# A one-core attention and mixture-of-experts kernel: the front reordered, small products grouped, half units and the last tiles in another order

## What is computed

```python
q, k, v = xn @ Wq.T + bq, xn @ Wk.T + bk, xn @ Wv.T + bv
qk = q @ k.T                                    # per batch, 1024 x 1024
theta = 0.5 + 0.2*sigmoid(qk) + 0.15*tanh(qk) + 0.1*relu(qk)
s = (softmax(theta) @ v) @ Wo.T + bo
e = argmax(xn @ Wr + br)                        # one of 8 experts for each row
y = gelu(xn @ W1[e] + b1[e]) @ W2[e] + b2[e]    # 256 -> 1024 -> 256
out = x + s * silu(y)
```

## Time and profile before

| | us |
|---|---|
| median of 3 runs | 537.14 |
| lowest and highest | 536.58, 537.76 |
| the profiled execution's own time | 537.1 |
| its span | 535.4 |
| TensorE busy in the span | 517.5 |
| VectorE, ScalarE, GpSimd busy | 408.2, 335.2, 195.4 |

### The profile page before, as it was taken

The page is one execution under the profiler, slowest core; times in us unless marked ns, Lnnn a source line. Parts: engine busy times, 40 slices in busy tenths (PEclk is TensorE's granted clock), DMA queues, the critical chain, the costliest instruction groups (busy, mean ns, idle before and its releaser), DMA issues.

```text
span 535.4 us, 10760 instructions
## 1 busy us (share of the span) xinstructions
PE 517.5 (97%) x3779; PEld 484.8 (91%) x3779; DVE 408.2 (76%) x810; ACT 335.2 (63%) x611; POOL 195.4 (36%) x230
## 2 busy tenths in 40 slices
PE   7998999999999999999999979999999999999996
PEld 6888899899989999899999969988899988999996
DVE  6897688955758855498555688758999999777896
ACT  3488778535536634266334464678777887877882
POOL 2226337931222212322112222004577685343443
PEclk9999999999999999999999999999999999999999
DMA  8942920027314731145311421005123232211121
GB/s 279 352 160 99 353 81 1 1 51 245 118 60 131 233 111 39 60 131 206 138 39 39 130 72 40 22 21 184 56 97 106 73 118 90 61 48 41 60 61 59
DMA packets 40323, 57.09 MB, mean 107 GB/s; under 512 B 3607, under 2 KB 35358, under 8 KB 39726
## 3 DMA queue, kind: packets, MB, share of 16 engines
q1 hardware_dynamic: 35020, 45.62, 25.5%
q0 software_dynamic: 3488, 9.47, 6.1%
q10 hardware_dynamic: 1762, 1.32, 0.8%
HBM read 40.68 MB, written 17.56 MB: 109 GB/s over the span
## 4 chain that ended last, share of the span: by engine, by line
PE 83%; DVE 8%; ACT 5%; issue 2%; DMA 2%; ACTq 0%; POOL 0%; POOLq 0%; DVEq 0%
PE ps L855 25%; PE ps L857 24%; PE ps L856 24%; PE ps L954 5%; DVE stats L1316 1%; PE ps L1137 1%; PE ps L1021 1%; DMA row<-xn_rows,unit_token 1%; ACT hid L731 1%; PE ps L1011 1%; DVE theta L1374 1%; DVE theta L1370 1%; DMA xn_all<-in_L_attn_x_dram 1%; ACT theta L618 1%; ACT theta L608 1%
## 5 line engine op out<-in xcount | busy, mean ns | idle before, releaser
L855 PE MATMUL ps<-v_hi,pT_hi 128*128 128x258 f32 x256 | 76.4, 298 | 2.2 <-issue 0.8
L856 PE MATMUL ps<-v_lo,pT_hi 128*128 128x258 f32 x256 | 72.4, 283 | 0.0
L717 ACT ACTIVATE hid<-ps,b_now 128x256 f32<-128x256 f32 x128 | 53.6, 471 | 30.0 <-PE ps L857 29.1
L857 PE MATMUL ps<-v_hi,pT_lo 128*128 128x258 f32 x256 | 72.2, 282 | 0.0
L1370 DVE SCALAR_TENSOR_TENSOR theta<-tanh_s,theta 128x512 f32<-128x512 f32 x64 | 48.8, 763 | 20.7 <-ACT tanh_s L609 20.0
L618 ACT ACTIVATE theta<-theta,neg_max 128x512 f32<-128x512 f32 x64 | 42.9, 721 | 29.9 <-DVE neg_max L1374 29.8
L855 PE MATMUL ps<-w_hi_even,hidT_h 128*128 128x256 f32 x200 | 58.1, 290 | 3.2 <-DVE hidT_l L1658 3.2
L739 ACT ACTIVATE g_sb<-y_sb 128x512 f32<-128x512 f32 x20 | 12.6, 632 | 71.7 <-DVE y_sb L1663 71.7
L499 POOL COPY unit_token<-sorted_token 128x2 int32 x19 | 3.7, 195 | 147.1 <-PE ps L1137 147.1
L857 PE MATMUL ps<-w_hi_even,hidT_l 128*128 128x256 f32 x200 | 56.6, 283 | 0.0
L856 PE MATMUL ps<-w_lo_even,hidT_h 128*128 128x256 f32 x200 | 56.6, 283 | 0.0
(11 more groups left out here) (248 smaller groups left out, 1648.6 us busy)
## 6 DMA issues: line engine op xcount, KB each, us to landing
w_raw_odd<-in_L_ffn_W_dram SPq DMA_DIRECT2D x10, 1024.0 KB, 5.7
w_raw_even<-in_L_ffn_W_dram SPq DMA_DIRECT2D x6, 1024.0 KB, 6.5
sorted_g<-g_sb SPq DMA_DIRECT2D x20, 256.0 KB, 2.2
xn_rows<-xn_all SPq DMA_DIRECT2D x4, 1024.0 KB, 6.1
x_tile<-in_L_attn_x_dram SPq DMA_DIRECT2D x32, 128.0 KB, 2.2
out_dram<-g_tile SPq DMA_DIRECT2D x32, 128.0 KB, 1.7
xn_all<-in_L_attn_x_dram SPq DMA_DIRECT2D x3, 1024.0 KB, 12.4
kept_xT<-passing_xT SPq DMA_DIRECT2D x2, 1024.0 KB, 4.1
```

The lines of the kernel that those rows point to most:

```text
L717: last = nc.scalar.activation(hid[:, j % 2, c * UNIT:(c + 1) * UNIT], ps[:, HID_BANK + j, c * UNIT:(c + 1) * UNIT], ACT.Gelu, bias=b1_now[ ...
L855: mm(dst, a_hi, b_hi, start=first, stop=False)
L856: mm(dst, a_hi, b_lo, start=False, stop=False)
L857: return mm(dst, a_lo, b_hi, start=False, stop=last)
```

## The change

**Front.** The three loads of the bias rows go from SyncE's queue to the head of ScalarE's. TensorE transposes the bias rows first and then does the eight identity products. A bias column (bk) is put beside Wk, so that M's product, 257 columns wide, gives the key offsets too (`offset_products` goes). `kappa` is a product and sum on VectorE over two rows that are loaded broadcast (`bq_all`, `bk_all`). `bo` is loaded broadcast, halved on GpSimd and added on VectorE, in place of a product. `first_u` starts u of the first half of batch 0 with the high parts, then the low part of M, then turns tiles 4 to 7, then the low part of xn. ScalarE normalises tiles 4 and 5 and copies woT and bv_wide, all of which VectorE did.

**Groups.** `route` is done for four tiles at once, `turn` two rounds at once, `invert` four tokens' tiles at once. The products themselves are the same.

**Half units.** The kept halves have semaphores of their own (`act_kept`, `dve_kept`). The hidden layer is handed over in four quarters instead of three pieces, and the high parts of the last two quarters are made on ScalarE. In all units, the wait for the next expert's weights (`w1_split`) moves from ahead of the branch into `hidden` and `half_rows`.

**Around tile 8.** Its exponentials move into `tile_8`, ahead of the last unit's gelus, with two table loads, and VectorE takes `thetas(9)` ahead of the last unit's bias.

**The end.** Tiles 30 and 31 join `ROUTING`. VectorE takes both halves of `thetas(31)` ahead of `transposed_parts(30)`, and TensorE puts the transposes of tile 31, in another bank, between the two halves of `values(30)`.

```diff
@@ constants, SyncE, ScalarE
-    ROUTING = (3, 4, 5, TPB)
+    ROUTING = (3, 4, 5, TPB, NT - 2, NT - 1)
-            for first, src in ((BQ, bq), (BK, bk), (BV, bv)):
-                sp.dma_start(bias_rows[first:first + DC, :], src.rearrange("(c p) -> c p", p=P)).then_inc(small_in, 16)
+            for kept, src in ((bq_all, bq), (bk_all, bk)):
+                sp.dma_start(kept[:, :], src.rearrange("(a d) -> a d", a=1).to_broadcast([P, D])).then_inc(pairs_in, 16)
...
+            for first, src in ((BQ, bq), (BK, bk), (BV, bv)):
+                act.dma_start(bias_rows[first:first + DC, :], src.rearrange("(c p) -> c p", p=P)).then_inc(small_in, 16)
             act.dma_start(wq_raw[:, :, :], chunked(Wq)).then_inc(wqk_in, 16)
@@ TensorE: groups
@@ -931,8 +974,9 @@
-                    if routed_batch is not None:
-                        route(routed_batch, 2 * q + i)
+                if routed_batch is not None and q % 2:
+                    for t in range(2 * q - 2, 2 * q + 2):
+                        route(routed_batch, t)
@@ scores
-                        if turned_batch is not None:
-                            turn(turned_batch, 2 * h + k)
+                        if turned_batch is not None and k == 0:
+                            turn(turned_batch, 2 * h)
+                            turn(turned_batch, 2 * h + 1)
@@ values
-                    if routed_batch is not None:
-                        route(routed_batch, i)
+                    if routed_batch is not None and i % 4 == 3:
+                        for t in range(i - 3, i + 1):
+                            route(routed_batch, t)
@@ TensorE: front
-            for ec in range(DC):
-                mm(ps[:, PT_BANK, 0:D], bv_wide[:, ec, :], woT[:, ec, :], start=ec == 0, stop=False)
-            mm(ps[:, PT_BANK, 0:D], ones[0:1, :], bo_row[:, :], start=False, stop=True).then_inc(const_done, 1)
...
+            for ec in range(DC):
+                last = mm(ps[:, PT_BANK, 0:D], bv_wide[:, ec, :], woT[:, ec, :], start=ec == 0, stop=ec == DC - 1)
+            last.then_inc(const_done, 1)
...
                 if n < 3:
-                    pe.wait_ge(turned_kept, 4 * n + 4)
+                    pe.wait_ge(turned_kept, 4 * n + 3)
...
-            values(n - 2, inverted=[[i] for i in range(TPB)], limited="ends")
-            values(n - 1, inverted=[[TPB + 2 * i, TPB + 2 * i + 1] for i in range(TPB)], limited="full")
+            values(n - 2, inverted=[range(i - 3, i + 1) if i % 4 == 3 else () for i in range(TPB)], limited="ends")
+            values(n - 1, inverted=[range(TPB + 2 * i - 2, TPB + 2 * i + 2) if i % 2 else () for i in range(TPB)], limited="full")
@@ ScalarE: half units
-                for s in range(1, 4):
-                    first, stop = HALF_STEPS[s]
-                    act.wait_ge(hid_done, u * 4 + 3 + stop // 8)
-                    for c in range(first, stop):
+                for s in range(4):
+                    act.wait_ge(hid_done, u * 4 + 3 + s // 2)
+                    for c in range(2 * s, 2 * s + 2):
...
+                wait_apart(act, act_kept, u * 2 + 2)
+                for s in range(2, 4):
+                    nc.scalar.activation(hidT_h[:, 2 * s:2 * s + 2, 0:P], half_gelus(s), ACT.Copy).then_inc(gelu_done, 1)
@@ ScalarE: tile 8
                 for h in range(2):
                     acts(TPB, h)
+                nc.scalar.activation(warm[:, 2:3], zeros[:, 0:1], ACT.Exp)
+                exps(TPB)
@@ TensorE: experts, the end
-                    if c == HC // 2:
-                        pe.wait_ge(w1_split, split)
+                    if c % (HC // 2) == 0:
+                        pe.wait_ge(w1_split, split - 1 + c // (HC // 2))
...
-                pe.wait_ge(w1_split, split - 1)
                 with pe.If(u0 < full):
...
-            weighted(NT - 2)
+
+            pe.wait_ge(half_s_ready, NT - 3)
+            values(NT - 2, blocks=range(0, TPB // 2))
+            pe.wait_ge(acts_done, (NT - 1) * 2)
             transposes(NT - 1)
+            values(NT - 2, blocks=range(TPB // 2, TPB))
             weighted(NT - 1)
@@ VectorE
-            biased(last_u, 1)
             thetas(TPB + 1)
+            biased(last_u, 1)
```

270 lines of the change are left out of this document (137 added, 133 removed).

## The result

The changed kernel takes 539.23 us (median of 20 runs, 536.77 to 541.09). The kernel before takes 536.90 us in the same comparison (20 runs, 536.36 to 537.76). The ratio is 1.0038, with a 95% interval from 1.0029 to 1.0047: slower by 2.3 us, where 5.6 us faster was forecast.

A forecast was written before the change was run, and what follows sets the result against it. TensorE was taken as the bound, so gains could come only from its few waits. Terms -2.1 (up to 66 us), -1.9, -0.9 and -0.8 sum to -5.7 us: 537.1 becomes 531.4, taken as 531.5, range 529.3 to 534.3.

The forecast's parts named there:

- The end, -0.8: Tiles 30 and 31: earlier `thetas(31)` brings `values(31)` to 528.1 instead of 528.86, despite a 0.75 us wait; -0.8 us.
- Half units, -1.9: Three uncovered half units: ScalarE's casts save 0.6 us at each of two, the moved wait 0.7 behind the third.
- lets TensorE start 0.7 us sooner: Behind the third half unit: branch done beforehand, first half's low part ready at 320.9, of a 1.08 us wait.
- Front, -0.4: Kernel start: first product at about 4.2 us, M 1.4 us late, yet `u_product(0, 2)` at 16.6 instead of 17.00.
- the front gives back: Rival: later first product keeps TensorE at its lower clock, M ends 11.5, nothing gained to 47 us; 532.8, chance 0.17.
- const -0.6: Constant: the product with `bo` goes, saving 0.62 us on TensorE; GpSimd's halving takes its place.
- tiles 0 to 2 -1.0: Up to 66 us: tile 2's turning at 45.6, gaps at `values(0)` and `values(1)` 0.4 us each, +0.1 at tile 3.
- Groups, 0.0: Small products: entering a group saves what leaving costs, 0.11 us each, so grouping gains nothing; ends +0.7 and -1.0.
- Behind the experts, -0.9: Around tile 8: the wait for `values(8)` goes, the second, ahead of `transposes(10)`, keeps its length but begins sooner; -0.9 us.
- ScalarE is the new bound: Rival, half units and tile 8: casts wait, table loads delay the last unit; -0.6 and 0.0, so 533.6; chance 0.12.

The follow-up runs named there:

- c4: Kernel before with the new end alone (tiles 30 and 31): 538.16 us against 536.94, ratio 1.0027.
- c1: Changed kernel with the whole front of the kernel before, `bo`'s product included: 538.10 us against 536.94 for the kernel before.
- c2: c1 with the last expert's loop on TensorE beginning at slot 128 of a code block instead of 0: 535.25 us against 536.94 before.
- a1: Changed kernel with Wq ahead of the bias rows, router loads on SyncE, broadcasts behind x's first batch: 537.62 us against 537.00 before.
- a2: a1 plus TensorE's old order at the start, and VectorE's bias-row copies behind its first statistics: 537.67 us against 537.00 before.
- a3: Changed kernel with the wait for the next expert's weights back ahead of the branch: 540.85 us against 537.00 before.
- e3: Kernel before with the changed front alone (loads, warm-up, first u products, offsets, constant): 539.15 us against 536.63.
- d1: Kernel before with the small products in groups alone: 535.30 us against 536.78, ratio 0.9969.
- e1: d3 with the last half unit's two casts back on VectorE: 532.82 us against 536.63 for the kernel before.
- c3: Kernel before with the new half units alone, the weights' wait staying ahead of the branch: 541.94 us against 536.94.
- f2: Kernel before with only the three bias-row loads moved to the head of ScalarE's queue: 541.76 us against 537.05.
- d3: c2 with the old end (tiles 30 and 31 as before): 534.01 us against 536.78 for the kernel before.
- e4: Kernel before with new half units, weights' wait inside the loop, last expert's loop at slot 128: 536.56 us against 536.63.
- d4: Kernel before with only the last expert's loop placed at slot 128 instead of 0: 536.68 us against 536.78.

## Why the prediction was wrong

- **The end, -0.8: it cost 1.2.** On TensorE the step was right: two waits became one, of 0.27 us where 0.75 was expected, and the last product gained 1.2 us between `transposes(10)` and the end. What failed is that I counted up to `values(31)` only. I never priced GpSimd, whose last product hangs on the end of `values(30)`: it moved 1.6 us later in c4 and 3.3 in the changed kernel, and with it the close of the program. I had no row for the drain, only the distance between GpSimd's last product and the span's end, 6.4 us, which I did not look at. Behind TensorE's last product the changed kernel loses 2.5 us, twice what it won ahead of it.
- **Half units, -1.9: the first two nearly as said, the third lost.** The second wait of 0.5 us is gone in both, which is worth 0.47 and 0.45 us (0.6 each forecast), and 0.30 us more are won at the first wait of the third. The step that failed is "lets TensorE start 0.7 us sooner". The 1.08 us of issue was put down to the wait for weights and a branch behind it. The limit was the fetch of the loop's block: c1 and c2 show it. The first half's low part was ready at 319.5, sooner than the 320.9 that I counted, and the unit still started at 321.69, as late as before. In place of a gain of 0.7 us came half clock, which cost 2.5 us in this profile. I had no rival for that. The branch is done beforehand, as I said, where no fetch stands in the way: in c2 the unit starts 0.1 us behind the split.
- **Front, -0.4: it was +3.0 at `u_product(0, 2)`.** The bias rows landed at 5.2 us and not at 4.2: the third load was issued by 1.97 us, sooner than my 2.4, and took 3.2 us where I had 1.7. But a1 and a2 show that this cost nothing. The miss, 3.4 us against the 16.6 of the forecast, comes from a step that wasn't there: what three small loads do to the loads behind them. I priced the moved loads at their issues, 0.5 us each, and M by TensorE alone; Wq landed 10.1 us into the span, and the second half of x at 13.1. I counted it as a gain that the statistics of x's second half no longer queue behind M, and they became what u waits for. The rival *the front gives back* had the right sign with the wrong order of events. M's eight passes did run at 1.2 GHz (3.58 us), but in a3 the same instructions took 1.98 us, and `u_product(0, 2)` came no sooner (20.24), since x landed late. In the Trainium skill, TensorE: Matmul & The Clock Gate, the part on the warm-up says that the moment differs from run to run, and these two profiles agree: the first product is at 5.22 us in one and 5.24 in the other, and M took 3.58 us in one and 1.98 in the other.
- **const -0.6 and tiles 0 to 2 -1.0.** The first is borne out: `scores(1)` is 2.04 us behind after 2.98. Of these 0.9 us, 0.62 are `bo`'s product. The rest of the 3 us is absorbed by 125 us, but only in part because a late TensorE waits less: with the new front alone (e3) 2.05 us are still there at expert 0, and the groups alone (d1) bring it 1.3 us forward. The two issue waits of 0.30 us that I meant to remove by waiting for the third kept bank are gone in d1 too, which waits for the fourth as before. The sum of the front and both parts up to 66 us was -2.1; with the old front (c1) `values(5)` is 0.3 us sooner than before and expert 0's first rows 1.1 us, no sooner than the groups alone make them. Neither part was run alone.
- **Groups, 0.0: alone they give 1.5.** The arithmetic of a group was right (0.112 each, of which leaving it costs 0.08 once). The mistake was to stop there: a group shifts where TensorE asks for things, and 0.65 + 0.3 + 0.3 us of waits went, 0.4 came. In the token groups 0.85 us came off, between the 0.0 and the good end of 1.0 that I gave.
- **Behind the experts, -0.9: alone 1.5.** The first wait went as said. The second went too, which I had kept. In the changed kernel it stayed, 0.98 us, since the half unit's casts held ScalarE up: my rival *ScalarE is the new bound* is true in the last half unit only, and e1 measures it at 1.0 us.

So the forecast of 531.5 us was not missed by one size: three terms had the wrong sign. The parts were costed one by one, and I summed them. Three pairs work against each other: the faster half unit and the fetch, ScalarE's casts and tile 9, TensorE's new order at the end and GpSimd. Each was visible as a queue or an engine with little slack behind the one that I looked at. Left open are why ScalarE's queue stalls behind small loads, and why the fetch in the kernel before began ahead of its wait's end while in a3 and c3 it began behind it.

## What to carry to other kernels

Price each moved DMA by what stands behind it on its queue, not by its issue. Look at every engine's last instruction, GpSimd's above all, before you take time off the last product. A gap called "issue" at a branch, or one put down to an engine that was done long before, may be a fetch of code: move the loop's place within its block before moving waits, and run parts alone, since here the whole was 2.3 us slower while the same parts, without the new front, the new end and two casts, and with one number changed, were 3.8 us faster.

## What the hardware showed that I had not expected

- Three loads of 1 KB at the head of ScalarE's queue made the 256 KB load behind them land after 8.4 us instead of 4.0 (f2), and later issues on it 1.4 to 1.7 us long (f2 and the changed kernel).
- A jump to a loop at the head of a block of TensorE's code took 2.5 to 3.3 us from the fetch to the first product; with the loop in the middle of a block the unit started 0.1 to 0.2 us behind the fetch in c2, d3, e1 and e4. In d4 it was 2.3 us, 0.59 of them behind TensorE's own last product.
- A gap of 2.41 to 5.02 us in steady work was followed by half clock for 3.41 or 6.83 us in all 8 profiles that had one there; gaps of up to 1.34 us were not.
- GpSimd's drain took 6.8 to 6.9 us and ended 6.06 us behind its last product, and the program could not close ahead of it.
